# A four-block transformer kernel on one core: another order of work at the opening of its causal attention stage

## What is computed

```python
x = _layernorm(x + _L0_attn_ref(x, ...))       # retention, 16 heads
x = _layernorm(x + _L0_ffn_ref(x, ...))        # 2 layers: windowed attention + gated MLP
x = _layernorm(x + _L1_attn_ref(x, ...))       # causal attention: the stage of this document
x = _layernorm(x + _L1_ffn_ref(x, ...))        # MLP of four matmuls

def _L1_attn_ref(x, Wk, Wq, Wv, Wo, bo, kln_g, kln_b, qln_g, qln_b):
    # EMB = 128, HEADS = 16, HEADSIZE = 8
    k = jnp.einsum('bte,fe->btf', x, Wk).reshape(B, T, HEADS, HEADSIZE)
    q = jnp.einsum('bte,fe->btf', x, Wq).reshape(B, T, HEADS, HEADSIZE)
    v = jnp.einsum('bte,fe->btf', x, Wv).reshape(B, T, HEADS, HEADSIZE)
    k = _layernorm(k, kln_g, kln_b)            # over the 8 values of one head
    q = _layernorm(q, qln_g, qln_b)
    scale = E ** (-0.25)
    q = q * scale
    k = k * scale
    dot = jnp.einsum('bihd,bjhd->bhij', q, k)
    causal = jnp.triu(jnp.ones((T, T), dtype=bool), k=1)
    dot = jnp.where(causal, -jnp.inf, dot)
    att = jax.nn.softmax(dot, axis=-1)
    out = jnp.einsum('bhij,bjhd->bihd', att, v).reshape(B, T, E)
    return jnp.einsum('bte,fe->btf', out, Wo) + bo
```

## Time and profile before

| | us |
|---|---|
| median of 3 runs | 1015.76 (1012.32 to 1017.3) |
| the profiled execution | 1016.58 |
| its span, first to last instruction | 1014.8 |
| PE, DVE, ACT, POOL busy | 858.4, 628.9, 516.6, 465.2 |
| first opening, end of narrowed to q_strips(0) | 293.71 to 304.76 |
| second opening | 794.33 to 805.38 |

### The profile page before, as it was taken

One profiled execution on the slowest core, in us unless ns is written; L12 is line 12 of the kernel. 1 busy time (PEld: TensorE's weight loads), 2 busy tenths in 40 slices (PEclk: granted clock), 3 DMA queues, 4 the chain that ended last, 5 costly groups with the idle time before them and its releaser, 6 DMA issues.

```text
span 1014.8 us, 19079 instructions
## 1 busy us (share of the span) xinstructions
PE 858.4 (85%) x6808; PEld 527.0 (52%) x6808; DVE 628.9 (62%) x1650; ACT 516.6 (51%) x1090; POOL 465.2 (46%) x497
## 2 busy tenths in 40 slices
PE   6876998799858788899897679987998478888998
PEld 3553676377635444444545447754676344444445
DVE  5888784678578666330279788746876775662202
ACT  3325775478635465632152267755775346655311
POOL 4767881388432322210176678615874314322101
PEclk9999999999987699999999899999999777988999
DMA  9101010011000000000000011001100000000000
GB/s 351 77 2 31 19 28 2 22 28 29 1 1 1 1 1 1 1 1 21 22 2 2 1 32 29 17 1 33 28 18 2 0 1 1 1 1 1 1 21 21
DMA packets 11630, 21.62 MB, mean 21 GB/s; under 512 B 1424, under 2 KB 6928, under 8 KB 11024
## 3 DMA queue, kind: packets, MB, share of 16 engines
q1 hardware_dynamic: 11248, 18.60, 6.2%
q10 hardware_dynamic: 288, 1.78, 0.5%
HBM read 11.87 MB, written 1.05 MB: 13 GB/s over the span
## 4 chain that ended last, share of the span: by engine, by line
PE 56%; DVE 20%; POOL 12%; issue 5%; ACT 5%; DMA 1%; POOLq 0%; SPq 0%; DVEq 0%; ACTq 0%
PE bank L841 11%; PE bank L389 10%; DVE arena L1238 4%; PE bank L752 4%; PE bank L649 3%; POOL arena L1764 3%; POOL arena L1774 3%; PE bank L831 3%; POOL arena L1779 3%; PE bank L601 3%; PE bank L719 2%; PE bank L738 2%; PE bank L508 2%; DVE arena L1084 2%; POOL arena L1733 2%
## 5 line engine op out<-in xcount | busy, mean ns | idle before, releaser
L389 PE MATMUL bank<-consts_sb,arena 128*128 128x128 f32 x1040 | 160.8, 296 | 80.4 <-DVE arena L1230 23.4
L389 PEld LDWEIGHTS bank<-consts_sb,arena 128*128 128x128 f32 x1040 | 124.3, 150 | 146.4 <-issue 64.8
L1382 ACT ACTIVATE arena<-bank 128x512 f32<-128x512 f32 (+2 forms) x300 | 146.2, 554 | 77.0 <-PE bank L389 27.7
L1681 POOL TENSOR_TENSOR rstd<-vareps,neghalf 128x1 f32<-128x1 f32 x96 | 53.1, 554 | 247.6 <-DVE vareps L900 247.6
L1238 DVE TENSOR_REDUCE arena<-bank 128x2 f32<-128x1024 f32 (+3 forms) x128 | 98.0, 818 | 48.4 <-PE bank L706 47.7
L1764 POOL TENSOR_TENSOR arena<-arena,neghalf 128x16 f32<-128x16 f32 x32 | 93.1, 2908 | 61.0 <-DVE arena L1086 61.0
L1831 POOL TENSOR_SCALAR_AFFINE_SELECT arena<-arena 128x256 f32<-128x256 f32 x128 | 50.9, 411 | 137.3 <-ACT arena L1593 134.1
L841 PE MATMUL bank<-arena,weights 128*128 128x512 f32 x256 | 111.9, 594 | 1.6 <-ACT arena L1649 1.6
L508 PE MATMUL bank<-weights,x_features 128*128 128x512 f32 x192 | 97.3, 621 | 13.7 <-DVE arena L1099 6.9
L1593 ACT ACTIVATE arena<-bank 128x1024 f32<-128x1024 f32 (+1 forms) x96 | 81.6, 881 | 26.6 <-PE bank L738 26.1
L1514 ACT ACTIVATE arena<-bank,arena 128x128 f32<-128x128 f32 x256 | 69.7, 383 | 35.9 <-DVE arena L1127 35.9
(11 more groups left out here) (178 smaller groups left out, 1614.6 us busy)
## 6 DMA issues: line engine op xcount, KB each, us to landing
arena<-arena SPq DMA_DIRECT2D x56, 130.0 KB, 2.3
weights<-wts_dram SPq DMA_DIRECT2D x1, 2824.0 KB, 19.5
weights<-wts_dram SPq DMA_DIRECT2D x1, 1817.0 KB, 13.5
weights<-wts_dram SPq DMA_DIRECT2D x1, 1561.0 KB, 9.6
arena<-x_dram SPq DMA_DIRECT2D x6, 256.0 KB, 3.3
consts_sb<-consts_dram ACTq DMA_DIRECT2D x1, 1226.5 KB, 6.8
out_dram<-x_inner SPq DMA_DIRECT2D x16, 64.0 KB, 1.5
consts_sb<-consts_dram SPq DMA_DIRECT2D x1, 768.0 KB, 4.8
```

The costliest lines, as they stand in the source:

```text
L389: mm = pe.transpose(bank[:, i * P:(i + 1) * P], src, ident)
L1382: return act.activation(dst, src, ACT.Copy)
```

## The change

Four edits in causal(), and buffer sq grows from 512 to 1024 columns so that it holds four tiles.

1. ACT takes the squares of tiles 0 to 3 first, then the four copies of queries and keys (2, 3, 0, 1), then the four of the values. Tiles 4 to 7 are squared, copied, values, in this order each.
2. place_high and low of the first four tiles go in the order 2, 0, 3, 1, in place of 0, 1, 2, 3.
3. Of fed_forward(1, 1) DVE does three tiles ahead of the steps, and the fourth, with the last two norms, behind maxima(0).
4. roots for tiles 4 to 7 is cut: its three opening instructions and one round at step 5, two rounds at step 6, behind that step's two maxima and ahead of scale(4).

```diff
-                    ("oS", 512), ("oN", G * D), ("cen", 1024), ("sq", 512), ("z", 512), ("ss", 32), ("t", 128),
+                    ("oS", 512), ("oN", G * D), ("cen", 1024), ("sq", 1024), ("z", 512), ("ss", 32), ("t", 128),
...
+        SCALED_FIRST, PLACED_FIRST = (2, 3, 0, 1), (2, 0, 3, 1)
+        ROOTS_AT = 6
...
-                for g in range(NT):
+                roots(True, 3)
+                for g in SCALED_FIRST:
+                    scale(g)
+                for g in PLACED_FIRST:
                     low(g)
-                fed_forward(1, 1)
-                fed_normed(G - 1)
+                dve.wait_ge(xb2_ready, 4)
+                for t in range(NT - 1):
+                    fed_tile(1, 1, t)
                 for s in range(END):
                     for f in fills_a(s):
                         maxima(f)
+                        if f == 0:
+                            fed_tile(1, 1, NT - 1)
+                            fed_normed(G - 1)
                         if f % NF == NF - 1:
                             negated(f // NF)
                     if s in STATS_AT:
                         stats3(STATS_AT[s])
                         if STATS_AT[s] == G - 1:
-                            roots()
+                            roots(True, 1)
+                    if s == ROOTS_AT:
+                        roots(False, 2)
                     for g in SCALE_AT.get(s, ()):
                         scale(g)
...
                 for g in range(NT):
-                    projected(g)
+                    squared(g)
+                for g in SCALED_FIRST:
+                    kept(g)
                 for g in range(NT):
+                    values_kept(g)
+                for g in PLACED_FIRST:
                     place_high(g)
```

82 lines of the change are left out of this document (44 added, 38 removed).

## The result

| | median us | lowest to highest | ratio to before, 95% |
|---|---|---|---|
| before, measured beside it | 1016.53 | 1012.03 to 1027.76 | |
| after the change | 1010.69 | 1000.75 to 1013.87 | 0.9896 [0.9858, 0.9934] |
| after, measured again | 1012.52 | 1001.2 to 1015.46 | 0.9958 [0.9927, 0.9988] |

Executions more than 1.5% above the fastest of their kernel are left out of the ratios, of all means and of the changed kernel's upper ends (of its 24 these are 1017.81, 1018.26 and 1020.66, merely its longest, and 1226.09, which at a granted clock of 0.664 is of another kind). The two sets are of one kernel and their ratios differ by 0.6%; the experiments show where that comes from.

The account below looks back on a forecast made before the run. PE and DVE were taken to bound the kernel, with PE idle for DVE at the opening and step 6. Gains of 1.4 + 1.96 = 3.36 us a pass, 6.7 for two, gave 1009.0 us from 1015.76; range 1003.5 to 1013.5.

Parts of the forecast that it names:

- Squares first: At the opening, ACT's squares ahead of its copies bring the fourth sum 0.36 us earlier; bounds 0.28 to 0.5.
- Placing: At the opening, placing tiles in order of readiness ends DVE's remainders 1.30 us earlier; bounds 0.8 to 1.67.
- The moved norm: Steps 0 and 1: fourth norm behind maxima(0) costs 0.3 us net, leaving 1.4 of the opening's 1.66; bounds 1.0 to 1.7.
- The rival that has the moved norm as the new wait: DVE sets the pace over steps 1 and 2, opening gives -0.4, time 1012.6; chance 0.18 shared with placing worth nothing.
- Roots over two steps: Six roots instructions leave the path to maxima(12); PE's step 6 fill comes 1.96 us earlier; bounds 1.3 to 1.96.
- DVE's cover: DVE's idle time behind step 6 falls from 3.27 to 1.31 us, hiding the roots' second half.
- The sum: Opening 1.4 plus roots 1.96 make 3.36 us a pass, 6.7 for two passes.
- The clock: PE's clock still falls at step 6, gain 0; rival that it stays up in one or both passes, chance 0.2.
- The price of 3.0 us a pass: Worth of PE's clock staying up at step 6: 1.2 us until DVE limits, plus 1.8 us up to 351.50.
- some 2 us: Spread expected in any median of three, from clock returns that fall here or there.
- The prediction's own sign of being wrong: Wrong if L738 still waits 4 us, steps 1 and 2 outgrow the opening's gain, or half-clock stretches differ by over about 5 us.

Follow-up runs that it names:

- norm ahead: Changed kernel with all four tiles of the fed rows and their norm ahead of the first maxima again; mean 1009.7 us, ratio to before 0.9926.
- filled pair: Changed kernel and kernel before, each with unread matmuls sized to PE's idle waits at the opening and step 6; means 1012.1 and 1018.0 us.
- the last kernel: Changed kernel with one unread 128x384 matmul in each head quad's 0.82 us second-pass wait, seven times a pass; mean 1003.8 us, ratio to before 0.9861.
- roots alone: Kernel before with only the roots split, one round at step 5 and two at step 6; mean 1018.1 us, ratio to before 0.9989.
- before filled to size: Kernel before with twelve unread matmuls in PE's opening wait and four at step 6; mean 1018.0 us, ratio to before 1.0003.
- overfilled opening: Unread matmuls longer than PE's opening wait: changed kernel 1026.0 us, with step 6 overfilled too 1025.4; kernel before with both overfilled 1039.6.
- opening alone: Changed kernel with the roots whole again at step 5; mean 1017.3 us, ratio to before 0.9996.
- placing alone: Kernel before with only the tile order 2, 0, 3, 1 for placing; mean 1018.4 us, ratio to before 1.0.

## Why the prediction was right, step by step

**Squares first**: forecast 0.36, measured 0.50, the upper end of its bounds. The sums follow one another at 0.67 us where I took 0.72. **Placing**: forecast 1.30, measured 1.44 alone. Together 1.94 against 1.66, so PE's wait was 9.11 and not 9.4. The estimate kept DVE's pace of before, 0.42 a tile; the lows of one tile and the next now stand 0.40 apart, and begin 0.1 sooner.

**The moved norm**: forecast a net cost of 0.3 us, measured 0.17 at the transposes of xM and 0.1 behind them. The steps came as forecast: maxima(0) alone at 308.24, forecast 308.24; the norm's end at 311.43, forecast 311.48; the transposes at 311.58, forecast about 311.55. The forecast left the 0.43 us later start of the stage out, so against the stage's start each is that much earlier. The opening is then worth 1.77 us by the transposes, against 1.4, a little above my upper bound. The rival that has the moved norm as the new wait is out: the norm ahead gives the same time within the error (1009.7 against 1009.0).

**Roots over two steps**: forecast 1.96, measured 1.94 to 1.96 in three kernels. The wait is 2.14 where 2.1 was forecast. DVE's cover behind it was 0.74 and not 1.31, since PE ran at full clock for some of the way to the next maxima: 4.34 us from the fill at 330.47 to 334.81, where it was 4.92.

**The sum** of 3.36 us a pass came as 3.0 (6.0 / 2) between the filled pair. In the profiled executions it came as 3.15 and 3.39 at step 10 of the first pass, and as 5.46 and 5.04 in the second. In the first pass that is right by two errors that cancel: the edits gave 3.9 up to step 6, and 0.3 more by the earlier return of the clock, and behind step 6 the wait for POOL and the clock, which comes back when it did before, take 0.9 to 1.05 back. In the second pass the clock's earlier return after the opening gives 1.5 to 2.0 where the sum had nothing, so there the sum is short by about 2. The forecast gave the opening's clock no term of its own.

**The clock** is where the working fell short. That it would fall at step 6 in spite of the shorter wait is right. The price of 3.0 us a pass for a clock that stays up there is borne out by the one pass in which it did, the first of the last kernel: 3.1 us. What the prediction didn't see is how hard it is to get: held up through the wait by fillings, the clock still fell for 13.7 us at the next waits, and nothing came of it.

The Trainium skill, "TensorE: Matmul & The Clock Gate", section "What's actually happening", has the half clock as the state of an engine that has been little busy, and activity as what releases it. By this rule, which the prediction weighed, halving the wait favours the full clock; the rows show 3.4 us at full clock in the middle of the spell, 334.43 to 337.84, and no more.

The step that failed is that I took the spells further on for constant. The one of before, at 408.6, had no place in the sum. They give a spread of 14 us from one execution to the next, and in the profiled executions they ate the gain of each edit alone. The "some 2 us" that I allowed in a median is small beside this: the counted executions of the two sets have means of 1006.8 and 1010.9. The prediction's own sign of being wrong, stretches at half clock that differ by more than about 5 us in sum, did appear in the means (108 against 122 us, 13 less before rounding), though not in the two profiles (92.2 against 95.6 in the causal stages).

So part of the hit is luck: the clock's changes had no term in the sum, and the place of a median depends on them. At 0.36 us for each, 13 us are 4.7 of the 8.2 us between the means; that is a rough split, since half clock in a wait is free. In the two profiles the opening's spells are 17.1 and 17.1 us, where they were 20.5 and 23.9. Half of these 10.2 us lies in the wait itself; the other half is what gave 0.3 us in the first pass and 1.5 in the second.

What stays open is what decides, among executions of the same program with the same waits, whether a late spell comes. The traces show them behind the same small waits, and not each time. In the first passes the clock that came back 59.1 to 59.5 us into the stage (placing, opening and roots alone, and before filled to size) fell again at step 10, and that which came back at 62.3 us or later did not, the kernels with an overfilled opening left out; in the second passes this order doesn't hold. Why opening alone and placing alone gave nothing in the mean stays open with it.

## What to carry to other kernels

Price an edit in the waits, but look up how the granted clock runs over the whole stage before turning this into a time: behind a wait of 0.8 us in an otherwise busy engine there can come a spell that costs 3.5 us. When an edit shows its gain in the trace and none in the time, compare the marks of each step against the stage's start, in every pass; the place where the gain goes in one piece names the cause in that execution. To test two kernels for their waits alone, fill the waits of both to size, and compare those.

## What the runs showed of the hardware that I had not expected

- Two profiled executions of one program, 1001.2 and 1013.3 us, have the same waits to 0.02 us at the places of the change, and 86 and 121 us with TensorE's clock at 1.2 GHz. The 35 us more cost 12.1.
- A us at half clock costs 0.30 to 0.35 us where PE works without long waits (3.5 for 10.2; 2.04 for 6.8), and nothing inside a wait (q_strips(0) at 14.60 us with the clock down in front of it, 14.62 with it up).
- Keeping PE busy through the wait of step 6 alone doesn't keep the clock up. In the first pass of two such kernels it fell 48.7 and 48.6 us into the stage for 13.7 us; without the filling it had fallen at 42.4 for 3.4 us and at 49.2 for 13.7.
- Filling waits of 0.82 us with work that nobody reads doesn't delay what waits (the second fill starts 1.31 us after the first, with the filling and without). Two of the fourteen fillings stood where the last quad of a pass has no such wait, and delayed its second fill by about 1 us. The mean is 5.3 us below the changed kernel's, with a standard error of 1.5.
- A 128x512 f32 matmul of the program is two instructions of 0.43 us at full clock.
